# The score row of a fused graph kernel: from four TensorE transposes to a round trip through DRAM

## What is computed

```python
h = relu(layernorm(x))
x = x + hypergraph(h, adj)      # incidence products, 256 -> 512, relu, layer norm, 512 -> 256
h = relu(layernorm(x))
# second layer
Xw = h @ Wv + bv
sj = Xw @ aw[:d, 0];  si = Xw @ aw[d:, 0]
e = leaky_relu(sj[:, None, :] + si[:, :, None] + ab[0], 0.2)
alpha = adj * exp(e)
transition = alpha / (alpha.sum(-1, keepdims=True) + 1e-12)
x = x + relu(h @ Wk0 + T(h) @ Wk1 + T(T(h)) @ Wk2 + biases)   # T: product with transition
```

## Time and profile before

| | us |
|---|---|
| median of 3 runs | 839.87 |
| lowest and highest of them | 839.61 and 844.78 |
| the profiled execution, its own time | 840.09 |
| span of that execution's instructions | 838.3 |

### The profile page before, as it was taken

How to read it: one execution, slowest core, us unless ns; L and a number is a source line. 1 busy time by engine, 2 the same in 40 slices (tenths; PEclk the granted TensorE clock), 3 DMA queues, 4 the chain that set the end, 5 groups by cost and what they waited for, 6 DMA issues and landing times.

```text
span 838.3 us, 16609 instructions
## 1 busy us (share of the span) xinstructions
PE 811.9 (97%) x5766; PEld 757.6 (90%) x5766; DVE 643.8 (77%) x1726; ACT 475.9 (57%) x1001; POOL 431.5 (51%) x596
## 2 busy tenths in 40 slices
PE   6888999999999999999999999999999999999997
PEld 5686999999999998999999899998989999899986
DVE  4769777878878787887778887777887877777565
ACT  3334738365573836657384674738457482754644
POOL 3657264573736547363654736365482736632242
PEclk9989999999999999999999999999999999999999
DMA  8131302204041220403122040312204031110001
GB/s 276 64 101 42 124 13 77 89 26 139 0 126 36 75 88 8 155 0 125 38 75 88 0 163 0 124 39 75 88 0 163 0 110 54 52 51 1 26 19 34
DMA packets 39807, 57.82 MB, mean 69 GB/s; under 512 B 2528, under 2 KB 20960, under 8 KB 39776
## 3 DMA queue, kind: packets, MB, share of 16 engines
q1 hardware_dynamic: 39776, 57.42, 20.7%
HBM read 49.03 MB, written 8.39 MB: 68 GB/s over the span
## 4 chain that ended last, share of the span: by engine, by line
PE 92%; DVE 4%; ACT 2%; issue 1%; DMA 1%; POOL 1%; SPq 0%; DVEq 0%
PE ps L699 86%; PE ps L886 3%; PE ps L831 1%; PE ps L875 1%; DMA r_sb<-in_adj 1%; DVE inct L1375 0%; POOL p_lo L421 0%; DVE inc L1038 0%; DVE st_x L1017 0%; ACT e_sb L575 0%; DVE r_sb L1171 0%; ACT h_f L510 0%; DVE x L1414 0%; ACT e_sb L581 0%; DVE st_r L1177 0%
## 5 line engine op out<-in xcount | busy, mean ns | idle before, releaser
L407 POOL TENSOR_TENSOR y<-y,bk_row 128x256 f32<-128x256 f32 x64 | 56.3, 909 | 207.9 <-DVE a_lo L1247 207.9
L699 PE MATMUL ps<-w_hi,part_a 128*128 128x256 f32 (+1 forms) x512 | 158.0, 344 | 4.9 <-DVE part_b L1234 2.7
L699 PE MATMUL ps<-w_lo,part_a 128*128 128x256 f32 (+1 forms) x384 | 124.3, 324 | 0.0
L699 PEld LDWEIGHTS ps<-w_hi,part_a 128*128 128x128 f32 x512 | 98.2, 192 | 17.6 <-issue 3.0
L699 PE MATMUL ps<-wk_hi,xt_hi 128*128 128x258 f32 (+1 forms) x256 | 89.4, 349 | 3.3 <-DVE xt_lo L1069 1.8
L699 PE MATMUL ps<-wk_hi,xt_lo 128*128 128x258 f32 (+1 forms) x256 | 86.7, 339 | 0.0
L699 PE MATMUL ps<-wk_lo,xt_hi 128*128 128x258 f32 (+1 forms) x256 | 86.6, 338 | 0.0
L699 PEld LDWEIGHTS ps<-w_lo,part_a 128*128 128x128 f32 x384 | 74.4, 194 | 5.8
L1241 DVE TENSOR_TENSOR e_sb<-e_sb,adjt_sb 128x512 f32<-128x512 f32 x64 | 44.2, 691 | 44.8 <-ACT e_sb L581 44.8
L411 POOL TENSOR_TENSOR xt_lo<-xl,xt_hi 128x256 fp32r<-128x256 f32 x60 | 57.0, 978 | 39.2 <-ACT xt_hi L655 39.1
L699 PE MATMUL ps<-w_hi,part_b 128*128 128x256 f32 x256 | 73.5, 287 | 0.0
(11 more groups left out here) (144 smaller groups left out, 2524.8 us busy)
## 6 DMA issues: line engine op xcount, KB each, us to landing
adjt_sb<-in_adj_t SPq DMA_DIRECT2D x16, 1024.0 KB, 5.3
adj_sb<-in_adj SPq DMA_DIRECT2D x31, 512.0 KB, 3.6
xin<-in_x SPq DMA_DIRECT2D x15, 512.0 KB, 4.5
out_dram<-x SPq DMA_DIRECT2D x15, 512.0 KB, 3.3
w_row<-in_adj SPq DMA_DIRECT2D x16, 256.0 KB, 3.5
e_sb<-in_w_t SPq DMA_DIRECT2D x2, 512.0 KB, 9.8
y<-in_wk SPq DMA_DIRECT2D x3, 256.0 KB, 4.5
xin<-in_x SPq DMA_DIRECT2D x4, 128.0 KB, 2.3
```

What stands on the lines that cost most here:

```text
L407: pool.tensor_tensor(y10[:, t, D:], y10[:, t, D:], bk_row[:, :], ALU.add).then_inc(po_y0, 1)
L699: return pe.matmul(dst, stationary, moving, start=first, stop=last, skip_group_check=True)
```

## The change

The row no longer goes through PE. DVE copies si into an SBUF tile with its two pairs of columns exchanged (so that the columns are in the order of the nodes), SP writes this 128x4 tile to a DRAM scratch, waits until it has landed, and reads it back as one row of 512 floats into every partition, into the first half of xl, which is free between the transposes of xl and g. There the element of node c*128+p lies at position p*4+c, and `spread` reads it with a stride of four floats. PE's y10 tiles have the same wait for each bank, and the last no longer waits for the scores. `eps_of_rows` is one instruction in place of two. On ACT and DVE the order changes: the four `nt_hi` and three of the `y10_out` come ahead of the scores' steps, and the four `lo_of_nt` ahead of `mult_a`.

```diff
+        si_row = xl[:, 0:2, :].rearrange("p c n -> p (c n)")
+        row_out = nc.dram_tensor("row_out", (P, TI), F32, kind="Internal").ap()
...
 SP, def step(s):
+                if s.prev:
+                    wait(sp, dv_si, at(s, -1))
+                    sp.dma_start(row_out, si[:, :]).then_inc(st_row, 16)
+                    wait(sp, st_row, dma_at(s, -1))
+                    row = row_out.rearrange("p c -> (p c)").rearrange("(a n) -> a n", a=1).broadcast_to([P, C])
+                    sp.dma_start(si_row, row).then_inc(ld_row, 16)
                 if s.prev2 and not s.prev:
...
 ACT, spread(t):
-                            wait(act, pe_si, at(s, -1))
+                            wait(act, ld_row, dma_at(s, -1))
...
-                        act.activation(e_sb[:, t, :], ps1[:, 0, :], ACT.Abs, bias=sj[:, bank:bank + 1]).then_inc(ac_abs, 1)
+                        act.activation(e_sb[:, t, :].rearrange("a (c p) -> a c p", c=TI),
+                                       si_row.rearrange("a (p c) -> a c p", c=TI), ACT.Abs, bias=sj[:, bank:bank + 1]).then_inc(ac_abs, 1)
 ACT, eps_of_rows():
-                        for h in range(2):
-                            act.activation(er[:, 2 * h:2 * h + 2], si[:, 2 - 2 * h:4 - 2 * h], ACT.Exp,
-                                           bias=ln_eps[:, :], scale=-MID).then_inc(ac_er, 2)
+                        wait(act, dv_si, at(s, -1))
+                        act.activation(er[:, :], si[:, :], ACT.Exp, bias=ln_eps[:, :], scale=-MID).then_inc(ac_er, 4)
 ACT, the order:
                 y10_out(0)
+                y10_out(1)
+                for t in range(TI):
+                    nt_hi(t)
+                y10_out(2)
                 spread(0)
                 spread(1)
+                exp(0)
                 spread(2)
-                exp(0)
+                exp(1)
+                y10_out(3)
                 spread(3)
-                nt_hi(0)
-                exp(1)
-                nt_hi(1)
-                y10_out(1)
-                nt_hi(2)
                 exp(2)
-                y10_out(2)
-                nt_hi(3)
+                y_hi(0)
                 hi_of_a(0)
                 exp(3)
-                y10_out(3)
-                y_hi(0)
                 hi_of_a(1)
 PE, y10_tile(t):
-                        if t < 3:
-                            wait(pe, dv_v, at(s, -2, t + 1))
-                        else:
-                            wait(pe, ac_abs, at(s, -1))
                         bank = (t + 1) % 4
+                        wait(pe, dv_v, at(s, -2, bank))
...
                 y10_tile(0)
-                if s.prev:
-
-                    wait(pe, dv_v, at(s, -2, 0))
-                    wait(pe, dv_si, at(s, -1))
-                    for t in range(TI):
-                        column = si[:, (t + 2) % 4:(t + 2) % 4 + 1].broadcast_to([P, P])
-                        last = pe.transpose(ps1[:, 0, col(t)], column, ident[:, :])
-                    last.then_inc(pe_si, 4)
                 y10_tile(1)
 DVE:
-                    dve.tensor_copy(si[:, :], ps0[:, :, D + 1]).then_inc(dv_si, 4)
+                    wait(dve, st_row, dma_at(s, -2))
+                    wait(dve, ac_er, at(s, -2))
+                    wait(dve, ac_abs, at(s, -2))
+                    dve.tensor_copy(si[:, 0:2], ps0[:, 2:4, D + 1])
+                    dve.tensor_copy(si[:, 2:4], ps0[:, 0:2, D + 1]).then_inc(dv_si, 4)
...
+                for t in range(TI):
+                    lo_of_nt(t)
                 mult_a(0)
-                lo_of_nt(0)
                 mult_a(1)
-                lo_of_nt(1)
-                lo_of_nt(2)
-                mult_a(2)
...
                 elif s.k != -1:
                     incidence(2)
-                    lo_of_nt(3)
                     incidence(3)
+                mult_a(2)
+                y_lo(0)
                 lo_of_a(0)
                 mult_a(3)
-                y_lo(0)
                 lo_of_a(1)
...
 DVE, g_out():
                     wait(dve, pe_xt, at(s, -1))
+                    wait(dve, ac_abs, at(s, -1))
```

More of the change, by code:

```diff
@@ L207, in build @@
         ld_b2 = sem("ld_b2")
+        st_row, ld_row = sem("st_row"), sem("ld_row")
         su_ones, su_pool, su_rows, su_pe, su_c = (sem(n) for n in ("su_ones", "su_pool", "su_rows", "su_pe", "su_c"))
@@ L214, in build @@
             sem(n) for n in ("pe_m", "pe_u", "pe_z", "pe_nt", "pe_y", "pe_g", "pe_o"))
-        pe_xt, pe_y2, pe_si, pe_y10, pe_p, pe_v = (
-            sem(n) for n in ("pe_xt", "pe_y2", "pe_si", "pe_y10", "pe_p", "pe_v"))
+        pe_xt, pe_y2, pe_y10, pe_p, pe_v = (
+            sem(n) for n in ("pe_xt", "pe_y2", "pe_y10", "pe_p", "pe_v"))
         ac_hf, ac_m, ac_u, ac_relu, ac_nt, ac_y, ac_g = (
```

## The result

The changed kernel takes 882.58 us (median of 4 runs, 881.12 to 883.68) against 840.63 (median of 4). The ratio is 1.0507, with a 95% interval from 1.0485 to 1.053: slower by 42 us. The profiled execution took 883.68, with a span of 881.7.

A forecast was written before the change was run, and what follows sets the result against it. PE was taken to bound the kernel (busy 97%). On the profiled 840.09 us, -6.2 (steady steps) + 1.2 (step 15) + 3.3 (step 16) + 2.2 (clock) = +0.5, so 840.6 us; range 836.5 to 864, with 837 to 847 for the forecast itself.

The forecast's parts named there:

- The prize: PE's four transposes of the scores' row: 0.44 us a step, 7.0 us over 16 steps, 6.2 in the 14 steady ones.
- ACT's own order: Steady step: ACT's earlier work, y10_out(2) last, sets the first spread's start at 436.4, 1.3 us after the row arrives.
- A cushion behind it: Steady step: about 0.6 us of delay on ACT before a step gains less than its 0.44.
- The stride as a rival: Spread's 16-byte-stride read costs 0.42 us more each; steady steps +0.9 each, 862.8 us in all; chance 0.37.
- A price of 2.2 us for the clock in step 16: Step 16: PE's idle of about 6 us lowers the granted clock behind it, costing 2.2 us, between 0 and 3.
- I take nothing: Spread's strided read on ACT: forecast adds zero, between no cost and 0.42 us a spread, 1.7 us a step.
- the bare read is nearest to 2.3: Read of the row into all partitions: taken as 2.3 us, from a 128 KB read at the program's start.
- The trip: From DVE's copy of si through store and read: 1.7 + 2.3 + 0.2 = 4.2 us, between 3.4 and 6.0.
- The rival of the late row: The 16-byte-piece store makes the trip 7 us; steady steps lose 0.7 each, 861 us in all; chance 0.10.
- the later loads had 1.3 us to spare: Steady step: incidence, behind mult_a(1) and the later half of adj, ready near 441.5 for m_stage at 442.8; spare 1.3.
- Step 15 was charged 1.2 us: Step 15: p_stage right behind the y tiles waits for later ACT and DVE, +1.2 us; the 0.44 is lost there.
- 3.3 was charged: Step 16: first spread 4.2 us behind the copy of si in place of 0.9, +3.3 us (bounds +2.5 and +5.1).

The follow-up runs named there:

- run without transfers: Changed kernel, but spread reads a row resident in SBUF (b1_row) contiguously, and the row's store and read are left out: 836.55 us, ratio 0.9969.
- run with the resident row: Changed kernel, but spread reads b1_row, in SBUF from the start, with the 16-byte stride, not waiting for the transfers, still made: 867.48 us, ratio 1.0331.
- run with the old ends: Changed kernel with steps 15 and 16 as before the change (four transposes, old order on ACT and DVE, no transfers): 867.69 us, ratio 1.0334.

## Why the prediction was wrong

**What held.** The prize, 0.44 us a step: 48.83 in place of 49.27, in 14 steps of the run without transfers. ACT's own order: it is ready for the row 5.6 us behind the copy (398.84 in the step shown), as forecast. A cushion behind it: contiguous and 0.6 us late, a step loses 0.10. The stride as a rival, with a chance of 0.37, though sized too small: 0.42 us for each spread at most (0.53 measured) and 0.9 us a step over before (1.31 in the run with the resident row). A price of 2.2 us for the clock in step 16; see below.

**The first step that failed: "I take nothing".** Between no cost and one more cycle for each element, the forecast took nothing, since no row showed a slow access pattern. But no row showed a pattern of this kind either, so the trace was silent, and the rule of the Trainium skill that stood beside it (Advanced Engine Details and Errata, SBUF Cachelines) named just this case. It costs 0.51 to 0.53 us a spread. By itself that is 1.3 us a step, 18 of the 42 us in the 14 steady steps, and with the late row 2.05, 29 us; in step 16 it is 2 more.

**The second: "the bare read is nearest to 2.3".** The trip was put at 4.2 us, from above 6.0. It took 6.6 in the step shown and 6.1 by the medians, 1.4 for the store and 4.7 for the read. The row that it was read from, 128 KB at the start of the program, has half the size (2.3 against 2.9 us), not one source for all partitions (0.5 us) and not a source just written (1.3 us). The upper end came from w_row, which has the size and the one source, and was short by 1.2 for the last reason alone. The rival of the late row expected the trouble in the 16-byte store, which was the one part that cost less than thought.

**The third: rivals priced one by one.** The stride gave 862.8 and the late row 861, each with the other in order. They are not exclusive, and both came. The cushion, forecast at 0.6 us and not measured by itself, is spent once: where the stride has used it up, the late row costs 0.85 in place of 0.10. The range ended at the single rival, and the time was 18.6 us behind it. The steps of the two were not summed right either: a delay of 1.7, less 0.6 of cushion and 0.44 gained, is 0.7 a step and not 0.9 (some 859 us in all), and one of 1.4 is 0.4 and not 0.7 (some 856). Each alone, they measured 867.5 and 851.1.

**The fourth: the later loads had 1.3 us to spare.** They hadn't always. With the row free and contiguous the transfers still cost 0.45 us a step, mostly in the three steps where half of adj is issued 4.8 us behind the copy and lands another 6.9 later; before it was 3.1 and 5.2.

**The fifth, in the ends.** Step 15 was charged 1.2 us, 2.9 with the stride; it lost 6.2. The waits on the parts of a are about what the rival of the stride foresaw, 2.8 us in four pieces in the changed kernel against 0.38 in one before; what was not foreseen is the clock behind them. Stretches of PE in the changed kernel (length; PE busy; granted clock, where 0.50 is the 1.2 GHz level and 1.00 the 2.4 GHz level; DMA share; GB/s), with the pieces of p_stage from its timeline ahead of them:

```profile
817.25 0.36 PE L706 MATMUL ps<-y_hi,a_hi 128*128 128x258 f32 x1 [0.95 <-ACT a_hi L617]
818.29 0.39 PE L706 MATMUL ps<-y_hi,a_hi 128*128 128x258 f32 x1 [0.56 <-ACT a_hi L617]
819.17 0.39 PE L706 MATMUL ps<-y_hi,a_hi 128*128 128x258 f32 x1 [0.38 <-ACT a_hi L617]
820.59 0.39 PE L706 MATMUL ps<-y_hi,a_hi 128*128 128x258 f32 x1 [0.92 <-ACT a_hi L617]
```

```profile
815.00:820.00 5.00, 2.78 (x17) 1.00 0.00 0
820.00:825.00 5.00, 4.41 (x23) 0.66 0.00 0
...
845.00:850.00 5.00, 5.00 (x26) 0.67 0.00 0
...
855.00:860.00 5.00, 0.00 (x0) 0.86 0.24 85
860.00:865.00 5.00, 1.27 (x6) 0.50 0.00 0
865.00:870.00 5.00, 5.00 (x30) 0.62 0.02 5
```

PE was busy for 2.78 of 5 us, and in the next stretch it was granted 0.66. Twenty-five microseconds later, behind two pauses of 1.19 and 0.56 us that the kernel before has as well (1.18 and 0.56), it fell again. At 0.66 and 0.67 of the clock, 5 us lose 1.7 each (an estimate from these rows). The second fall is not the change's doing alone: the run with the old ends, in which the same instructions and pauses stand there, had 0.75 and then 0.91 in the two 5 us stretches at this place and took 1.5 us longer from copy to copy than the kernel before, which kept 1.00.

In step 16 the row was there 5.7 us behind the copy of si (849.73 to 855.42, by the timelines below) in place of 0.9, +4.8 where 3.3 was charged; four long spreads add 2.1. That leaves some 2.2 of the 9.1 us for the clock, granted at 0.50 and 0.62 behind PE's idle of 9.45 us, where 2.2 was forecast for an idle of 6; it is a remainder, and no run has it alone. Timelines of DVE, ACT and PE:

```profile
849.58 0.15 DVE L1224 COPY si<-ps 128x2 f32<-128x2 f32 x1
```

```profile
855.42 2.29 ACT L584 ACTIVATE e_sb<-xl,sj 128x512 f32<-128x512 f32 x2 [6.28 <-DMA xl<-row_out]
```

```profile
863.73 0.55 PE L706 MATMUL ps<-y_hi,a_hi 128*128 128x258 f32 x1 [9.45 <-DVE a_lo L1247]
```

## What to carry to other kernels

Where the trace has no row for an access pattern, it says nothing about it: if a rule names the pattern, put the cost and not zero into the sum, or carry both ends as equal cases. Sum a latency chain by what is special in each link (who wrote the source, how many read it, what is queued behind), and price rivals that can happen together also as a pair, because they draw on one cushion. And when a bound engine is relieved by 0.9% in each step, look first at the steps where nothing hides the longer route: here the last two cost 15 us, more than twice the 6.2 that all the others could gain.

## What the hardware showed that was not expected

- ACT, 128x512 float32 in SBUF: 712 to 716 ns contiguous, 749 with a read in steps of 8 bytes, 1225 in steps of 16 bytes, and 1218 if the write (in steps of 512 bytes) and not the read jumps.
- Reading 256 KB into 128 partitions: 2.9 us with a source for each, 3.4 with one 2 KB row of adj for all, 4.5 to 4.7 (medians) if that row was written just before, in either of two places, and 3.4 to 3.8 again in the steps where the store before it had taken a microsecond longer.
- Storing 2 KB to DRAM: 1.4 us in 128 pieces, 8.3 us in 512.
- The granted clock fell to 0.66 behind a stretch in which PE was busy for 2.78 of 5 us, without any single idle of a microsecond; and behind the same two pauses it fell in one kernel (0.75) and not in another (1.00) that is the same there.
